# Attention sandwich kernel: a head pair's slot in two stretches instead of three, with seven ring tiles

## The chip, the cores and the metric

The kernel runs on one core of one Trainium2 chip. The metric is the time of one launch on the device, in microseconds (us). Before the change three runs gave 1004.36, 1004.42 and 1005.59 us, so the median is 1004.42 us. One more execution was profiled.

## The reference

The input x has 4 batches of 1024 tokens of 128 numbers, all fp32. Two sublayers follow each other, each wrapped in layer norms and a residual:

```python
x = x + layernorm(attention(layernorm(x)))
x = x + layernorm(ffn(layernorm(x)))
# attention: layer norm with gain and bias, then 16 heads of 64
q, k, v = (xn @ w + b for each)              # 1024 x 64 per head
scores = q @ k.T / 8
scores = where(tril(ones, k=-1), -inf, scores)   # a query sees keys at or after its own place
h = softmax(scores) @ v
out = h @ w0 + b0 + residual
# ffn: 8 experts of rank 16; gates from the first token of each sequence of 64, top 2, softmax
```

The attention is nearly all of the work: 4 batches x 8 pairs of heads = 32 head pairs, each with a triangle of 1024 x 1024 scores for two heads.

## The kernel before

One loop of 32 **slots**, one for each head pair t. The engines are programmed by hand, each with its own instruction list, and are tied by semaphores. The lists of all engines follow the same tables (`TILES`, `T_STEPS`, `BLOCKS`, `S_STEPS`, `ORDER`, `fills`), which therefore set the order of the whole kernel.

For each pair the scores are computed twice. **First scores** (`score`, L649, called S steps, nine a pair): q by k in one product, into banks of the tile `sc` (three PSUM banks, taken in rotation, one for each of the two heads of a step). VectorE takes row maxima from them (`maxima`, L1156 where the mask must be added, L1159 elsewhere) and they are thrown away. The maxima become a shift for each query: `least_of_two` (DVE L1167), `shifts` (POOL L446 and L447), a transpose on TensorE ("m", L755), a copy on ScalarE (L1015), two DMAs that move it into `shift_row` (`move_shift`, L342). They are made a pair or two ahead. **Second scores** (`score_t`, L678 and L683, called T steps, ten a pair): transposed, with high and low parts of q and k (three products), the shift added by a product with `shift_row` (L678). They go to the two PSUM tiles `st0` and `st1` alternately, so step s needs the exponential of step s-2 to be done. ScalarE takes the exponential (`exponentials`, L969) into an SBUF tile. TensorE multiplies the tile with v (`weigh`, L698, called W here) into `po`, and GpSimd adds the tiles up for the softmax's sums (`add`, L467). S steps are written here S0 to S8 and T steps T0 to T9; S0' and so on are those of the pair after the next one's first steps.

Of the ten tiles of a pair, eight go to a ring of five tiles, and the first tile of each half (steps 0 and 7) goes straight to `total`, where the others are added onto it in place. That is why `add` waits for the W of step 0 or 7.

A slot has three **stretches**. Each is: T steps with S steps between them (the letters of `ORDER`), then **fills** (other products, whose results other engines take away), then the W of the stretch's T steps. With the names of `fills`:

| stretch | T and S steps | fills | W of |
|---|---|---|---|
| 0 | S3 T0 S4 T1 T2 S5 | sum(t-1), q(t+2), out(t-2) | T0 to T2 |
| 1 | S6 T3 T4 S7 T5 T6 S8 | k(t+2) | T3 to T6 |
| 2 | S0' T7 S1' T8 T9 S2' | m(t+1), v | T7 to T9 |

"sum" turns GpSimd's totals into one row (L708), which goes through four DMAs to VectorE's reciprocal (L1337), through DRAM and two DMAs (`spread_sums`, L355 and L359) into `inv_row`, and there GpSimd's `normalise` (L474) makes `o_norm`; "out" (L761) multiplies that with w0, and VectorE adds it to `acc` (L1222). Once a batch there are further fills, z, u, logit, mix and up, which turn the normed input of the next batch or do the second sublayer of the last one, and layer norms whose statistics VectorE makes with `norm_stats` (L1129 to L1136) at fixed places of the slots. SyncE issues all DMAs from one queue in program order: in a slot the sums, the reciprocals, the spread, loads of x and the store of a result where there are any, and last the shift.

## Time and profile before

| what | value |
|---|---|
| median of three runs | 1004.42 us |
| the profiled execution | 1005.35 us |
| its span, first to last instruction | 1003.5 us |
| TensorE busy | 963.6 us, 96% |
| VectorE busy | 645.9 us, 64% |
| ScalarE busy | 538.0 us, 54% |
| GpSimd busy | 703.1 us, 70% |
| mean granted TensorE clock | 0.993 |

The profiled execution took 0.93 us more than the median, of which 1.85 us lie outside its span. A busy share is an average over the whole program; what the change does is decided inside a slot, so slots are read one by one. In the timeline a row gives the start, the duration, the engine, the line and the operation; rows of the same kind are merged, and x is their number. Matmuls overlap each other, so what a step takes on TensorE is the distance from its start to the next step's start.

### The profile page before, as it was taken

What the parts mean: (1) busy time and instruction counts of PE and PEld (TensorE: products, weight loads), DVE (VectorE), ACT (ScalarE), POOL (GpSimd) and SP (SyncE); (2) the same over time, 40 slices, a digit from 0 to 9 for tenths busy, and PEclk for the clock granted to TensorE, in tenths of its full rate; (3) what the DMA queues carried; (4) which work ended last, traced back from release to release, by engine and by line L of the source; (5) the groups of instructions that cost most, each with busy time, mean ns of one, the idle gap of its engine ahead of it and who ended that gap; (6) DMA issues with size and microseconds to landing.
All of it is one profiled execution on the core that took longest, in us unless ns stands there. A gap on an engine that the chain in (4) does not pass through costs nothing.

```text
span 1003.5 us, 20485 instructions
## 1 busy us (share of the span) xinstructions
PE 963.6 (96%) x7677; PEld 603.8 (60%) x7682; DVE 645.9 (64%) x1935; ACT 538.0 (54%) x732; POOL 703.1 (70%) x519
## 2 busy tenths in 40 slices
PE   8999999999999999999999999999999999999995
PEld 3465666666666665666665566566666656666563
DVE  4766566565567667657667757656665765756377
ACT  6245655564544565665455565565545546455443
POOL 7266767687666768876576977776687776777752
PEclk9899999999999999999999999999999999999999
DMA  4001101001111100012001210000101210000010
GB/s 114 22 2 24 23 2 23 24 23 44 23 23 26 20 23 23 23 23 45 17 8 23 65 24 23 23 17 8 44 22 24 64 24 14 12 23 23 23 44 21
DMA packets 61809, 26.94 MB, mean 27 GB/s; under 512 B 39056, under 2 KB 53776, under 8 KB 61712
## 3 DMA queue, kind: packets, MB, share of 16 engines
q1 hardware_dynamic: 61712, 25.64, 10.9%
q8 instruction: 61, 1.00, 0.4%
q14 instruction: 36, 0.29, 0.1%
HBM read 22.76 MB, written 2.35 MB: 25 GB/s over the span
## 4 chain that ended last, share of the span: by engine, by line
PE 75%; POOL 11%; DVE 6%; ACT 5%; issue 3%; DMA 0%; POOLq 0%; ACTq 0%; DVEq 0%
PE po L698 21%; PE st L683 15%; PE st L614 9%; POOL total L467 8%; PE sc L649 8%; PE st L761 5%; PE st L678 5%; ACT ring L969 3%; PE sc L708 3%; PE st L629 2%; DVE sc L1156 2%; PE st L630 1%; PE st L631 1%; POOL moments L438 1%; DVE stats L1129 1%
## 5 line engine op out<-in xcount | busy, mean ns | idle before, releaser
L467 POOL TENSOR_TENSOR total<-total,ring 128x1024 f32<-128x1024 f32 (+1 forms) x313 | 539.4, 1723 | 251.6 <-PE po L698 208.6
L1156 DVE CUSTOM_DVE_ANT_0 sc<-sc,key_mask 128x512 f32<-128x512 f32 (+1 forms) x496 | 230.3, 521 | 144.8 <-PE sc L649 142.4
L969 ACT ACTIVATE ring<-st 128x1024 f32<-128x1024 f32 (+1 forms) x256 | 228.7, 919 | 166.3 <-PE st L683 148.3
L1159 DVE TENSOR_REDUCE least<-sc 128x1 f32<-128x512 f32 x268 | 170.2, 677 | 74.6 <-PE sc L649 70.6
L698 PE MATMUL po<-ring,v_sb 128*64 128x512 f32 (+3 forms) x1280 | 210.7, 467 | 0.0
L683 PE MATMUL st<-q_high,k_low 64*128 64x512 f32 (+3 forms) x768 | 177.0, 447 | 0.0
L698 PEld LDWEIGHTS po<-ring,v_sb 128*64 128x64 f32 x1280 | 86.7, 137 | 129.2 <-issue 124.1
L649 PE MATMUL sc<-k_high,q_high 64*128 64x512 f32 (+3 forms) x768 | 135.3, 383 | 11.3 <-DVE least L1156 5.2
L683 PE MATMUL st<-q_low,k_high 64*128 64x512 f32 (+3 forms) x768 | 136.9, 343 | 0.0
L683 PE MATMUL st<-q_high,k_high 64*128 64x512 f32 (+3 forms) x768 | 136.3, 342 | 0.0
L649 PEld LDWEIGHTS sc<-k_high,q_high 64*128 64x128 f32 x768 | 68.8, 185 | 82.4 <-issue 65.9
L678 PE MATMUL st<-shift_row,pick 64*128 64x512 bf16 (+3 forms) x640 | 105.6, 316 | 0.2 <-ACT total L969 0.2
L969 ACT ACTIVATE total<-st 128x1024 f32<-128x1024 f32 x64 | 65.7, 1027 | 54.5 <-PE st L683 54.5
L983 ACT COPY o_raw<-po 128x512 f32<-128x512 f32 x64 | 37.4, 585 | 90.7 <-PE po L698 90.4
L683 PEld LDWEIGHTS st<-q_high,k_high 64*128 64x128 f32 x768 | 76.3, 185 | 6.7
L1208 DVE SCALAR_TENSOR_TENSOR q_low<-st,bias_col,q_high 128x1024 fp32r<-128x1024 f32 x32 | 41.1, 1283 | 60.6 <-ACT q_high L1007 58.5
L683 PEld LDWEIGHTS st<-q_high,k_low 64*128 64x128 f32 x768 | 78.3, 190 | 0.0
L683 PEld LDWEIGHTS st<-q_low,k_high 64*128 64x128 f32 x768 | 77.0, 187 | 1.7
L474 POOL TENSOR_TENSOR o_norm<-o_raw,inv_row 128x1024 f32<-128x1024 f32 x31 | 74.0, 2386 | 3.5 <-DMA inv_row<-sums_dram 3.5
L1156 DVE DVE_READ_ACCUMULATOR2_ANT least<- 128x1 f32 x496 | 69.9, 141 | 0.0
L698 PE MATMUL po<-total,v_sb 128*64 128x512 f32 x256 | 69.3, 620 | 0.0
L761 PEld LDWEIGHTS st<-w_sb,o_norm 128*128 128x128 f32 x480 | 58.0, 191 | 4.2 <-ACT ring L969 1.9
(170 smaller groups left out, 1281.2 us busy)
## 6 DMA issues: line engine op xcount, KB each, us to landing
inv_row<-sums_dram SPq DMA_DIRECT2D x62, 256.0 KB, 4.0
x_a<-x SPq DMA_DIRECT2D x4, 512.0 KB, 5.2
sums<-sums_row SPq DMA_DIRECT2D x124, 2.0 KB, 2.1
x_b<-x SPq DMA_DIRECT2D x3, 512.0 KB, 5.5
out<-res_b SPq DMA_DIRECT2D x3, 512.0 KB, 4.5
ring<-w_pairs SPq DMA_DIRECT2D x1, 1152.0 KB, 7.3
shift_row<-shift_t SPq DMA_DIRECT2D x64, 4.0 KB
x_a<-x SPq DMA_DIRECT2D x2, 256.0 KB, 3.2
```

Source lines behind the costliest of these rows:

```text
L467: nc.gpsimd.tensor_tensor(so_far, so_far, tile_of(n, s)[:, :, col:col + w], ALU.add).then_inc(s_add, 1)
L474: nc.gpsimd.tensor_tensor(o_norm[:], o_raw[n % 2][:], inv_row[:], ALU.mult).then_inc(s_norm, 1)
L614: last = nc.tensor.matmul(dst, low if part == 1 else high, (x_high if part else x_low)[:, tokens], start=(part == 0), stop=(part == 2))
L649: last = nc.tensor.matmul(banks[h][:, col:col + w], q_high[n % 3][rows[h], i * P:(i + 1) * P], k_high[n % 3][rows[h], k0:k0 + w], start=Tr ...
L678: nc.tensor.matmul(st[s % 2][:, h, col:col + w], picked[rows[h], :], shift_row[n % 2][rows[h], q0:q0 + w], start=(i == 0), stop=False)
L683: last = nc.tensor.matmul(st[s % 2][:, h, col:col + w], k[rows[h], keys], q[rows[h], queries], start=False, stop=(part == 2 and i + 1 == l ...
L698: last = nc.tensor.matmul(po[h * D:(h + 1) * D, 0:w], v_sb[(n // 2) % 2][:, j, c0:c0 + D], tile_of(n, s)[:, h, col:col + w], start=(s in F ...
L761: last = nc.tensor.matmul(at("out", n, 0)[:, t * P:(t + 1) * P], o_norm[:, t * P:(t + 1) * P], w0_sb[:, n % PAIRS, :], start=True, stop=True)
L969: nc.scalar.activation(tile_of(n, s)[:, :, 0:w], st[s % 2][:, :, 0:w], ACT.Exp, scale=SCALE).then_inc(s_exp, 1)
L1156: last = nc.vector.tensor_tensor_reduce(bank[:, col:col + w], bank[:, col:col + w], key_mask[:, 0:w], -1.0, 3e38, ALU.add, ALU.min, least[ ...
L1159: last = nc.vector.tensor_reduce(least[:, h, a:a + 1], bank[:, col:col + w], AX.X, ALU.max, negate=True)
L1208: nc.vector.scalar_tensor_tensor(out=low[n % 3][:], in0=src, scalar=bias_col[:, n % PAIRS, w:w + 1], in1=high[n % 3][:].bitcast(fp32), op0 ...
```

## The change

The slot has two stretches. Nothing that is computed changes.

| stretch | T and S steps | fills | W of |
|---|---|---|---|
| 0 | S3 T0 S4 T1 T2 S5 T3 T4 S6 T5 S7 T6 S8 | sum(t-1), q(t+2), k(t+2) | T0 to T6 |
| 1 | S0' T7 S1' T8 T9 S2' | m(t+1), v, out(t-2) | T7 to T9 |

The ring has seven tiles. Tile 0 goes to the ring too, and GpSimd's first addition writes tile 0 + tile 1 to a `total_first` of its own; tile 7 (`IN_PLACE`) goes to the single `total_second` and is added onto in place. `normalise` comes before the additions of tiles 8 and 9 on GpSimd, and `shifts` after all additions of stretch 0. The fills z, u and up take two `sc` banks each, one after the other, instead of an `st` tile. On VectorE a stretch's `take` comes before its layer norm statistics.

```diff
-    T_STEPS = [range(0, 3), range(3, 7), range(7, 10)]
+    T_STEPS = [range(0, 7), range(7, 10)]
...
-    ORDER = ["STSTTS", "STTSTTS", "STSTTS"]
+    ORDER = ["STSTTSTTSTSTS", "STSTTS"]
...
-    FIRST_ORDER = ["TSTSTSS", "STSTTSTS", "STSTTS"]
-    RING = 5
+    FIRST_ORDER = ["TSTSTSTSTSTSTSS", "STSTTS"]
+    RING = 7
...
+    IN_PLACE = 7
+    IN_RING = [s for s in range(STEPS) if s != IN_PLACE]
...
         if g == 0:
-            if 2 <= t < N:
-                found.append((("out", t - 2, 0), y))
-            if 1 <= t < N:
-                found.insert(0, (("sum", t - 1, 0), "sc"))
...
+            if t >= 1:
+                found.append((("sum", t - 1, 0), "sc"))
+            if t + 2 < N:
+                found += [(("q", t + 2, 0), x), (("k", t + 2, 0), y)]
+            if t == N - 1:
+                found.append((("out", t - 2, 0), x))
...
+            if t + 2 < N:
+                found.append((("v", (t + 2) // 2, t % 2), x))
+            if 2 <= t < N - 1:
                 found.append((("out", t - 2, 0), y))
+            if before and i == 5:
+                found.append((("z", c + 1, 0), "sc"))
...
         def tile_of(n, s):
-            if s in FIRST:
-                return total[:, FIRST.index(s), n % 2]
-            return ring[:, ring_count(n, s) % RING]
+            return total_second[:] if s == IN_PLACE else ring[:, ring_count(n, s) % RING]
...
             def add(n, s):
                 half = half_of(s)
                 pool.wait_ge(s_exp, STEPS * n + s + 1)
-                pool.wait_ge(s_pv, STEPS * n + FIRST[half] + 1)
+                if half:
+                    pool.wait_ge(s_pv, STEPS * n + IN_PLACE + 1)
...
+                    nc.gpsimd.tensor_tensor(so_far, tile_of(n, 0) if s == 1 else so_far, tile_of(n, s)[:, :, col:col + w],
+                                            ALU.add).then_inc(s_add, 1)
...
+                    if g == 1 and t >= 1:
+                        normalise(t - 1)
                     for s in T_STEPS[g]:
                         if s in SUMMED and (t, s) not in LAST_SUMS:
                             add(t, s)
-                        if s == 4 and t < N - 1:
-                            shifts(t + 1)
-                    if g == 1 and t >= 1:
-                        normalise(t - 1)
+                    if g == 0 and t < N - 1:
+                        shifts(t + 1)
...
-                    if t >= 0:
-                        place = 3 * i + g
+                    for use, bank in fills(t, g):
+                        take(use, bank)
+                    for place in ((3 * i, 3 * i + 1), (3 * i + 2,))[g]:
```

TensorE's list, inside slot 8, from T2 on. L678 and L683 are a T step, L649 an S step, L708 the sum, L614 a projection. Before:

```order
L678 MATMUL st<-shift_row,pick 128x512 x2
L683 MATMUL st<-q_high,k_low 128x512 x2
L683 MATMUL st<-q_low,k_high 128x512 x2
L683 MATMUL st<-q_high,k_high 128x512 x2
L649 MATMUL sc<-k_high,q_high 128x512 x2
L708 MATMUL sc<-total,ones 32x512 x4
L614 MATMUL st<-x_low,wqk_high 128x512
L614 MATMUL st<-x_high,wqk_low 128x512
L614 MATMUL st<-x_high,wqk_high 128x512
```

The same place now, where L701 and L706 are a T step and L672 is an S step:

```order
L701 MATMUL st<-shift_row,pick 128x512 x2
L706 MATMUL st<-q_high,k_low 128x512 x2
L706 MATMUL st<-q_low,k_high 128x512 x2
L706 MATMUL st<-q_high,k_high 128x512 x2
L672 MATMUL sc<-k_high,q_high 128x512 x2
L701 MATMUL st<-shift_row,pick_masked 128x128 x2
L701 MATMUL st<-shift_row,pick 128x128 x2
L706 MATMUL st<-q_high,k_low 128x256 x2
L706 MATMUL st<-q_low,k_high 128x256 x2
L706 MATMUL st<-q_high,k_high 128x256 x2
L701 MATMUL st<-shift_row,pick 128x512 x2
```

After S5 the short T3 and then T4 follow at once, where there were the sum, a projection, out and the W of three tiles.

GpSimd's list in slot 9, from the shift on, before (L446 and L447 are the shift, L467 an addition, L474 `normalise`):

```order
L446 CAST shift<-least 128x2x8
L447 TENSOR_TENSOR shift<-least,shift 128x2x8
L467 TENSOR_TENSOR total<-total,ring 128x1024
L467 TENSOR_TENSOR total<-total,ring 128x2x384
L467 TENSOR_TENSOR total<-total,ring 128x2x128
L474 TENSOR_TENSOR o_norm<-o_raw,inv_row 128x1024
L467 TENSOR_TENSOR total<-total,ring 128x2x384
```

And in slot 8 now, where L462 and L463 are the shift, L488 an addition, L454 and L455 a layer norm's root, L496 `normalise`:

```order
L488 TENSOR_TENSOR total_first<-total_first,ring 128x2x384
L488 TENSOR_TENSOR total_first<-total_first,ring 128x2x128
L462 CAST shift<-least 128x2x8
L463 TENSOR_TENSOR shift<-least,shift 128x2x8
L454 TENSOR_TENSOR moments<-moments,minus_half 128x8
L455 TENSOR_TENSOR moments<-moments 128x8
L496 TENSOR_TENSOR o_norm<-o_raw,inv_row 128x1024
L488 TENSOR_TENSOR total_second<-total_second,ring 128x2x384
```

The shift now stands behind all additions of tiles 1 to 6, and `normalise` ahead of those of tiles 8 and 9.

VectorE's list at the end of slot 9, from the maxima of S2' on. Before, the out's addition had been done in stretch 0 (L1159 is a maximum, L1129 to L1136 are `norm_stats`):

```order
L1159 TENSOR_REDUCE least<-sc 128x1 x2
L1129 BN_STATS stats<-acc 128x6 x4
L1132 BN_AGGR moments<-stats 128x2 x4
L1135 TENSOR_SCALAR moments<-moments 128x4
L1136 TENSOR_SCALAR moments<-moments 128x4
```

Now, where L1178 is a maximum, L1245 the addition of out, L1148 to L1155 `norm_stats`, and L1175 the maxima of the next slot's S3:

```order
L1178 TENSOR_REDUCE least<-sc 128x1 x2
L1245 TENSOR_TENSOR acc<-st,acc 128x1024
L1148 BN_STATS stats<-acc 128x6 x4
L1151 BN_AGGR moments<-stats 128x2 x4
L1154 TENSOR_SCALAR moments<-moments 128x4
L1155 TENSOR_SCALAR moments<-moments 128x4
L1175 ISA sc,least<-sc,key_mask 128x384
```

The statistics stand behind the addition of out, which is filled late in the slot, and directly ahead of the next slot's first maxima.

## Rows read from the trace of the kernel before

**Rows 1.** Waits: engine line <- for whom: us in total, times, longest.

```profile
PE sc L649 <- DVE least L1156: 5.2, 5, 1.7
PE st L678 <- DVE k_low L1208: 3.5, 4, 1.1
PE sc L708 <- POOL total L467: 3.0, 4, 1.1
```

**Rows 2.** Windows, slot 8: us, then busy us of each engine.

```profile
276.93:305.35 28.42, 28.10 (x231) 17.70 (x229) 18.13 (x55) 14.34 (x17) 19.87 (x14) 1.00 0.10 21
```

**Rows 3.** Timeline of TensorE, slot 8, stretch 0: start, us, engine, line.

```profile
276.93 0.51 PE L649 MATMUL sc<-k_high,q_high 64*128 64x384 f32 x4
277.28 0.39 PE L678 MATMUL st<-shift_row,pick 64*128 64x512 bf16 x2
...
278.50 0.49 PE L649 MATMUL sc<-k_high,q_high 64*128 64x512 f32 x2
...
280.67 0.43 PE L649 MATMUL sc<-k_high,q_high 64*128 64x512 f32 x2
281.03 1.06 PE L708 MATMUL sc<-total,ones 128*32 128x512 f32 x8
...
285.39 1.08 PE L698 MATMUL po<-total,v_sb 128*64 128x512 f32 x4
```

**Rows 4.** Timeline of TensorE, slot 8, stretch 1 and the start of 2.

```profile
288.12 0.50 PE L649 MATMUL sc<-k_high,q_high 64*128 64x256 f32 x4
288.46 0.23 PE L678 MATMUL st<-shift_row,pick_masked 64*128 64x128 bf16 x2
...
288.99 0.39 PE L678 MATMUL st<-shift_row,pick 64*128 64x512 bf16 x2
...
289.92 0.40 PE L649 MATMUL sc<-k_high,q_high 64*128 64x512 f32 x2
290.15 0.23 PE L678 MATMUL st<-shift_row,pick_masked 64*128 64x128 bf16 x2
...
292.25 0.45 PE L649 MATMUL sc<-k_high,q_high 64*128 64x384 f32 x4
292.63 0.50 PE L614 MATMUL st<-x_low,wqk_high 128*128 128x512 f32 x1
...
294.22 3.23 PE L698 MATMUL po<-ring,v_sb 128*64 128x256 f32 x20
297.38 0.50 PE L649 MATMUL sc<-k_high,q_high 64*128 64x512 f32 x2
```

**Rows 5.** Timeline of TensorE, slot 31, which has no S steps: T1 and T2.

```profile
948.49 0.39 PE L678 MATMUL st<-shift_row,pick 64*128 64x512 bf16 x2
...
949.77 0.39 PE L678 MATMUL st<-shift_row,pick 64*128 64x512 bf16 x2 [0.18 <-ACT total L969]
```

**Rows 6.** Timeline of VectorE, slot 8: the maxima of S6, first head.

```profile
288.66 0.43 DVE L1156 CUSTOM_DVE_ANT_0 sc<-sc,key_mask 128x256 f32<-128x256 f32 x1 [1.38 <-PE sc L649]
...
289.39 0.14 DVE L1156 DVE_READ_ACCUMULATOR2_ANT least<- 128x1 f32 x1
```

**Rows 7.** Timeline of VectorE and GpSimd: statistics beside GpSimd's work.

```profile
303.63 0.17 DVE L1135 TENSOR_SCALAR moments<-moments 128x4 f32<-128x4 f32 x1
...
332.66 0.93 DVE L1135 TENSOR_SCALAR moments<-moments 128x4 f32<-128x4 f32 x1
...
331.19 2.37 POOL L474 TENSOR_TENSOR o_norm<-o_raw,inv_row 128x1024 f32<-128x1024 f32 x1
```

**Rows 8.** Timeline of SyncE, slot 8; landing of its spread; a page line: KB, us.

```profile
290.43 0.37 SPq L355 DMA_DIRECT2D sums_dram<-inv_sums  x1
293.14 1.31 SPq L359 DMA_DIRECT2D inv_row<-sums_dram  x2
...
DMA to landing us min/median/max: 3.7/3.8/4.0
...
sums<-sums_row SPq DMA_DIRECT2D x124, 2.0 KB, 2.1
```

171 lines of the change are left out of this document (89 added, 82 removed).

## The prediction, written before the changed kernel ran

> **What bounds the kernel now.** First the page: TensorE is busy 96% of the span, the others 54 to 70% (the table of the profile). So the question is what TensorE's list waits for. The waits view answers for the whole program: TensorE's largest waits are 5.2 us on VectorE's maxima, 3.5 us on VectorE's k_low and 3.0 us on GpSimd's totals [rows 1]. Then one ordinary slot, the eighth: 28.42 us, TensorE busy for 28.10 [rows 2]. Its timeline shows steps that follow each other at the pace of the products. Only one place in it waits: S4 starts 1.57 us after S3, where S3 and T0 take 0.35 and 0.93, so 0.3 us are a wait for VectorE [rows 3]. TensorE's own pace sets the end, then, and a change helps by giving it less to do and hurts by making it wait.
>
> **What it no longer has to do.** Each change of the kind of product costs a little. An S step between T steps takes 0.23 (289.92 to 290.15); S6 behind a W takes 0.34, S5 ahead of the sum 0.36 [rows 3, 4]. A projection is 1.59 between an S step and a W, and six matmuls at 0.23 are 1.38 [rows 4]. The W of 1536 columns takes 2.73 us and that of 1792 takes 3.16 (285.39 to 288.12, 294.22 to 297.38), so a column takes 1.68 ns, 1536 of them 2.58, and 0.15 us are fixed [rows 3, 4]. Where stretches 0 and 1 become one, one each of these goes: 0.11 + 0.13 + 0.21 + 0.15 = 0.6 us a slot. In the 29 slots from 1 to 29 that is -17.4 us. The number of matmuls stays, and out, k, u, z and up only move. The Trainium skill (TensorEngine Tiling (Array Packing), Key Properties) says that a change of the tiling mode drains TensorE; the sum would be the same, as the rows give the price and the page has none.
>
> **What it now waits for in the long stretch.** Seven T steps and six S steps follow each other, where the fills and W of 7 us used to let the other engines catch up. Two loops decide.
>
> ScalarE: a T step needs the exponential of the step two before. Slot 31 has no S steps, and there T1 takes 1.28 us where a T of this width takes 0.93 (288.99 to 289.92), so the loop is 0.93 + 1.28 = 2.21 us [rows 4, 5]. T1, T2 and S5 are 2.09, so T3 waits 0.12. T2, S5 and T3 (0.53 [rows 4]) are 1.69, 1.81 with that wait, so T4 waits 0.4. Later T steps are 2.3 us or more apart. Together 0.52.
>
> VectorE: S(k+1) needs the maxima of the first head of S(k), and the sum needs those of S7's second head. S3 to S4 is 1.57 [rows 3], and S6 has the same two pieces to a head (0.73 from its first maximum to the read of the second [rows 6]). S6 takes 0.12 less than S3, so S7 is 1.45 behind S6, while S6 and T5 (1.06) are 1.29: wait 0.16. An S step that was waited for takes 0.31 and not 0.23, another 0.08. S7 to S8 is about even. The sum comes one S step (0.38) after S8 and needs the head that VectorE takes after the one S8 needed, some 0.65 later: wait 0.27. Together 0.52, an estimate from these rows.
>
> So 1.04 us a slot, x 29 = +30.2. The bounds: nothing, if VectorE and ScalarE run ahead, and 1.6 if each T step must wait for a whole exponential. I take the value worked out, as the loop of 2.21 is measured.
>
> **Waits that go.** The q and k fills now stand 5.7 us of W ahead of T7, and VectorE takes them ahead of its statistics, so the k_low waits (3.5) go. The sum comes 9.4 us into the slot and not 4.1, so GpSimd's totals are ready (3.0). The waits for maxima (5.2) were VectorE being late at the head of a slot, for z or for statistics; I take them out and count what stands there now below. -11.7 [rows 1].
>
> **VectorE late at the head of a slot.** This is the largest new term after the long stretch. In slots 8, 9, 11, 16, 17, 19, 25 and 27 VectorE has statistics in the last stretch, now behind the out it must add. Taking S0' as zero, from the rows of slot 8: the rest of the scores is 3.6 us, m and v 1.9, out 1.9, so out is filled at 7.4, added at 8.8, and the two TENSOR_SCALAR of the statistics come at about 10.1; the next slot starts at 9.7 and its maxima should start at 10.3. GpSimd stands before `normalise`, which needs inv_row: the reciprocal ends at 2.0, the spread is issued 2.7 after the store of the reciprocals (290.43 to 293.14), its second DMA 0.7 after its first and lands 4.0 after its issue [rows 8], at 9.4. So `normalise` runs from 9.4 to 11.8. A TENSOR_SCALAR takes 0.17 us with GpSimd idle, but the one at 332.66, within `normalise`, takes 0.93 and ends with it [rows 7]. Here it would start 0.7 into it and end at 11.9, and the maxima start at 12.0 in place of 10.3. S4 is then 1.7 us late: x 8 = +13.6. Both ends: 0 if out or inv_row come at another time, 3.6 if the second TENSOR_SCALAR also waits for the addition that follows.
> By the Trainium skill (SBUF — State Buffer, Who interferes with whom) a tensor_scalar in a two-port mode and GpSimd shut each other out for a whole instruction, and whoever comes first wins. By that rule the wait is the remainder of `normalise`, as I counted; had VectorE come first, it would be nothing.
> In stretch 0 of the slots with two statistics in a row (six) VectorE ends some 0.45 late for S0': +2.7, from nothing to three times that.
>
> **z.** Three times a program z is filled at a slot's end, now in `sc` banks that the next S3 needs. ScalarE's two passes in halves and VectorE's end about 3.7 us behind the fill, and only 2.3 of W cover it: +4.2, from 2 to 6.
>
> **The shift's DMA.** The reciprocal is behind S0', so SyncE has issued the spread only at 6.1 after S0' (4.7, and 1.3 for its two issues [rows 8]), and m is ready at 4.6: the shift leaves 1.5 us later than it could. Its second DMA, 0.7 later, lands at 8.9 if it takes the 2.1 of the small DMAs of the sums [rows 8], and T0 needs it at 10.1. In ordinary slots 1 us is to spare. In slots 6, 14 and 22 a load of x of 512 KB stands between; if the shift's packets come behind it, T0 is late by 0.85, of which 0.3 is the wait of S4 that was there anyway: +1.7. In slots 9, 17 and 25 the same falls under the late maxima. In the Trainium skill (DMA: Bandwidth & Descriptors, Queues, rings and completion order) descriptors of a ring are taken in order, which gives this wait; no row here has a shift behind a load, and without the order it would be nothing.
>
> **Ends.** Slot 0: fewer kinds, VectorE-bound before and after: -0.5. Slots 30 and 31 have hardly any S steps and no projections; there m waits for GpSimd's shift, T0 to T6 run at the exponentials' pace, and the last sums start later: +3.1, from 0 to 7.
>
> **Sum.** -17.4 + 30.2 - 11.7 + 13.6 + 2.7 + 4.2 + 1.7 - 0.5 + 3.1 = +25.9. The profiled execution took 1005.35, 0.93 above the median, so 1031.2 there and 1030 against the median of 1004.42.
>
> **Rivals.** (1) Faster: TensorE's own time goes on binding. Its place is T2 to T4 and S6 to the sum. If VectorE and ScalarE run ahead there, neither 30.2 nor the statistics' 13.6 and 2.7 arises: 1005.35 - 17.4 - 11.7 + 4.2 + 1.7 - 0.5 + 3.1 = 984.8. For it: 46% of ScalarE's and 36% of VectorE's time is idle, and GpSimd's additions no longer wait for a W. Against it: the loop of 2.21 is latency and not load. It turns faster than before where the waits of the stretch are under 0.15 us a slot with the other terms as they are. Chance 0.13.
> (2) The statistics do not meet `normalise`: 1031.2 - 16.3 = 1014.9. For it: the meeting rests on two chains that end 0.7 us apart. Chance 0.2.
> (3) GpSimd becomes the bound. `normalise`, three additions of the last half and six of the first now run in one piece from 9.4 after S0', and only then the shift: GpSimd's work of a slot is 19.87 us in 14 instructions [rows 2], some 21.5 with the gaps between them, and it starts about where the slot does, while m needs the shift at 22.9. If it is 1 us later than m each slot, +28: 1059. Against it: 1.4 us to spare. Chance 0.09.
> (4) The change doesn't do what it says: not seen, the lists have the order of the table.
> The forecast has 0.58.
>
> **Range and chances.** The forecast's own range is 1018 to 1042: 0.25 us a slot either way in the long stretch is 7 us, and the statistics give as much. With rival 2 and the near side of rival 3 it is 1006 to 1045; rival 1 lies outside. Two us, 0.2%, is what a measurement of this kernel tells from no change. Faster takes rival 1, 0.13; the same 0.04, from rival 2's low end and a milder rival 1; slower 0.83.
>
> **What would show it.** In the changed profile an ordinary slot is about 28.9 us. From S3 to the sum it is 9.3 to 9.6 us, with T4 0.4 late and the sum on VectorE's maxima in the waits view. The merged W is 5.7 us, and no k_low wait is left. In the slots after those eight S4 starts over 3 us behind S3, with a TENSOR_SCALAR of 1.5 to 2 us ahead of it. The prediction is wrong if S3 to the sum is under 8.8 us, if those S4 are in time, or if m waits for GpSimd.

## The result, and the profile after

The changed kernel took 1044.25, 1047.69, 1048.45 and 1050.17 us, median 1048.07; beside it the kernel before took 1005.0 (1004.36 to 1005.9). The ratio is 1.042, with a 95% interval of 1.040 to 1.044. The forecast was 1030 and its range ended at 1045: the direction was right, the size was not. The profiled execution is the fastest of the four, 1044.25 us with a span of 1042.5, so the profile explains 39.0 us of span and not the last 4 us between the medians.

The waits view of TensorE after (columns as in [rows 1]):

```profile
PE st L701 <- DMA shift_row<-shift_t: 14.1, 8, 4.1
PE st L701 <- ACT ring L987: 8.9, 33, 0.6
PE sc L672 <- DVE least L1175: 5.7, 4, 2.2
PE st L652 <- ACT ring L987: 4.7, 25, 0.2
PE st L772 <- POOL o_norm L496: 3.6, 1, 3.6
PE st L701 <- ACT total_second L987: 3.5, 1, 3.5
PE sc L672 <- DVE x_low L1235: 3.5, 3, 1.2
PE sc L672 <- DVE least L1178: 2.6, 5, 0.8
PE sc L827 <- ACT shift_t L1033: 2.4, 3, 0.8
PE sc L830 <- ACT shift_t L1033: 2.3, 3, 0.8
```

The k_low waits of [rows 1] and those of the sum for GpSimd's totals are gone. At the top stands a wait that the kernel before did not have: T0 waiting for the shift's DMA, eight times (in slots 2, 7, 10, 15, 18, 23, 26 and 29).

The windows of slot 8, as [rows 2]:

```profile
280.44:309.29 28.85, 28.12 (x231) 17.96 (x229) 17.70 (x51) 14.20 (x17) 19.65 (x13) 1.00 0.08 20
```

The ordinary slot went from 28.42 to 28.85 us; 28.9 was forecast. The timeline of TensorE in its long stretch, to be read against [rows 3, 4]:

```profile
280.44 0.50 PE L672 MATMUL sc<-k_high,q_high 64*128 64x384 f32 x4
...
284.16 0.42 PE L672 MATMUL sc<-k_high,q_high 64*128 64x512 f32 x2
284.55 0.23 PE L701 MATMUL st<-shift_row,pick_masked 64*128 64x128 bf16 x2
...
285.47 0.39 PE L701 MATMUL st<-shift_row,pick 64*128 64x512 bf16 x2 [0.22 <-ACT ring L987]
...
286.40 0.40 PE L672 MATMUL sc<-k_high,q_high 64*128 64x256 f32 x4
...
287.87 0.50 PE L672 MATMUL sc<-k_high,q_high 64*128 64x512 f32 x2
...
289.87 0.62 PE L731 MATMUL sc<-total_first,ones 128*32 128x512 f32 x2
```

From S3 (280.44) to the sum (289.87) it is 9.43 us, within the 9.3 to 9.6 of the forecast; T4 (285.47) is the step that waits for an exponential, as forecast. S6 to S7 (286.40 to 287.87) is 1.47, the pace of VectorE's maxima (1.45 forecast).

So the loss is elsewhere, at the heads of some slots. TensorE in slot 18, where it was worst, and the windows with the granted clock (the number after the five engines):

```profile
582.49 0.50 PE L672 MATMUL sc<-k_high,q_high 64*128 64x384 f32 x4
587.05 0.61 PE L701 MATMUL st<-shift_row,pick 64*128 64x512 bf16 x2 [4.07 <-DMA shift_row<-shift_t]
```

```profile
585.30:592.20 6.90, 5.15 (x26) 3.40 (x28) 1.29 (x2) 2.05 (x2) 4.64 (x4) 0.51 0.07 21
...
401.02:404.43 3.41, 3.12 (x14) 2.19 (x16) 2.19 (x8) 0.56 (x1) 3.03 (x3) 0.50 0.02 5
889.90:896.00 6.10, 3.92 (x34) 2.64 (x32) 5.40 (x16) 2.62 (x4) 5.54 (x4) 1.00 0.01 3
```

TensorE stood 4.07 us for the shift, up to 587.05. From 585.3, while it stood, to 592.2 the clock was at half, 1.2 of 2.4 GHz, so T0 took 1.68 us in place of 0.93. Slot 18 took 35.08 us. In slot 12, where TensorE had waited 2.03 us for the maxima, it was at half for 3.4 us (second row); at the head of slot 28, after 2.17 us, it stayed at full (third row).

SyncE's list ahead of slot 18 (start, duration of the issue) shows why the shift is late:

```profile
577.77 2.51 SPq L375 DMA_DIRECT2D inv_row<-sums_dram  x2
580.33 0.59 SPq L403 DMA_DIRECT2D out<-res_b  x1
580.97 0.58 SPq L346 DMA_DIRECT2D x_b<-x  x1
581.64 1.97 SPq L358 DMA_DIRECT2D shift_row<-shift_t  x2
```

The spread waits for the late reciprocal, then a store and a load of 512 KB go first. In the trace the packets of the store and the load run from 582.2 to 586.2, those of the shift from 586.1 to 586.4.

The statistics met `normalise` in two of the eight slots only. VectorE and GpSimd at the end of slot 11, where they did, and VectorE at the end of slot 9, where they did not (as [rows 7]):

```profile
398.09 2.22 DVE L1154 TENSOR_SCALAR moments<-moments 128x4 f32<-128x4 f32 x1
...
397.92 2.37 POOL L496 TENSOR_TENSOR o_norm<-o_raw,inv_row 128x1024 f32<-128x1024 f32 x1 [3.80 <-PE po L721]
```

```profile
338.53 0.17 DVE L1154 TENSOR_SCALAR moments<-moments 128x4 f32<-128x4 f32 x1
...
338.69 0.57 DVE L1175 CUSTOM_DVE_ANT_0 sc<-sc,key_mask 128x384 f32<-128x384 f32 x1
```

At 398.09 the small instruction came 0.17 us behind `normalise` and ended with it, 2.22 us later. In slot 9 it came 29.2 us after the slot's first product, 0.55 us ahead of `normalise` (339.08).

Last, slot 30. ScalarE there stood 8.76 us for VectorE's gate work, whose small instructions stood in turn beside GpSimd's additions:

```profile
971.35 0.40 ACT L1014 ACTIVATE up_gated<-up_sb,gate 128x128 f32<-128x128 f32 x1 [8.76 <-DVE gate L1213]
```

```profile
967.12 2.26 DVE L1208 TENSOR_TENSOR gate<-gate 128x8 f32<-128x8 f32 x1
969.42 0.17 DVE L1209 TENSOR_TENSOR gate<-gate,own 128x8 f32<-128x8 f32 x1
```

The account, each term of the forecast beside what the two profiles show. Slots 1 to 29 went from 842.63 to 876.38 us; the measured terms are sums over the slots in which the thing stands, less an ordinary slot. The waits that go are not measured by themselves: that row is what is left over in slots 1 to 29, whatever its cause.

| term | forecast, us | profile, us |
|---|---|---|
| long stretch less the kinds that go, 29 x 0.43 | +12.8 | +12.5 |
| shift's DMA, half clock after it included | +1.7 | +17.1 |
| statistics beside GpSimd at a slot's end | +13.6 | +5.4 |
| z in `sc` banks | +4.2 | +3.7 |
| m ahead of logit and mix | none | +3.0 |
| two statistics in stretch 0 | +2.7 | +2.8 |
| waits that go | -11.7 | -10.8 (the remainder) |
| up to the end of slot 0 | -0.5 | -3.0 |
| slots 30, 31 and the tail | +3.1 | +8.3 |
| sum | +25.9 | +39.0 |

The -3.0 is the luck of two executions and not the change. It stands ahead of S3 of slot 0, in windows with nearly the same work (columns as in [rows 2], before and then after):

```profile
0.00:48.77 48.77, 43.28 (x191) 20.02 (x195) 29.81 (x82) 19.71 (x33) 24.00 (x61) 0.93 0.25 70
```

```profile
0.00:45.84 45.84, 39.88 (x193) 18.88 (x194) 29.82 (x82) 19.71 (x33) 24.21 (x62) 1.00 0.27 74
```

In the profile of the kernel before the clock was at half from 23.6 to 30.4 us, in that of the changed kernel it was not; in e1 and e2 below, which begin like the changed kernel, it was, and S3 of slot 0 starts at 48.66 and 48.87. Without this difference the two spans would be some 42 us apart, an estimate from these rows, near the 43 us between the medians. The other executions have no trace, so that it accounts for the rest is not shown.

### The profile page after: what moved, and what is told of

It is laid out like the page before. It is cut to its first block, busy times and chain, and to the rows that moved or that the text cites. A ratio compares the mean times of both kernels' runs of the same rounds, so it can differ in the third digit from the quotient of the medians.

```text
span 1042.5 us, 20498 instructions
## 1 busy us (share of the span) xinstructions
PE 967.0 (93%) x7682; PEld 612.7 (59%) x7682; DVE 653.7 (63%) x1938; ACT 536.3 (51%) x741; POOL 705.4 (68%) x519
## 3 DMA queue, kind: packets, MB, share of 16 engines
q1 hardware_dynamic: 61712, 25.64, 10.8%
## 4 chain that ended last, share of the span: by engine, by line
PE 62%; DVE 15%; ACT 7%; DMA 6%; POOL 4%; issue 3%; SPq 2%; POOLq 0%; ACTq 0%; DVEq 0%
PE po L721 18%; PE st L706 11%; PE st L637 9%; DVE sc L1175 8%; PE sc L672 5%; ACT ring L987 5%; PE st L701 4%; PE st L784 4%; PE sc L731 3%; DMA shift_row<-shift_t 3%; DMA sums_dram<-inv_sums 3%; PE st L652 2%; SPq L375 1%; POOL total_first L488 1%; PE po L841 1%
## 5 line engine op out<-in xcount | busy, mean ns | idle before, releaser
L488 POOL TENSOR_TENSOR total_first<-total_first,ring 128x1024 f32<-128x1024 f32 x188 | 343.9, 1829 | 25.5 <-POOL total_first L488 0.9
L987 ACT ACTIVATE ring<-st 128x1024 f32<-128x1024 f32 (+1 forms) x288 | 258.6, 929 | 130.5 <-PE st L706 124.8
L1175 DVE CUSTOM_DVE_ANT_0 sc<-sc,key_mask 128x512 f32<-128x512 f32 (+1 forms) x496 | 229.5, 521 | 64.0 <-PE sc L672 62.5
L1178 DVE TENSOR_REDUCE least<-sc 128x1 f32<-128x512 f32 x268 | 170.3, 678 | 129.2 <-PE sc L672 127.7
L721 PE MATMUL po<-ring,v_sb 128*64 128x512 f32 (+3 forms) x1408 | 232.7, 478 | 0.0
L496 POOL TENSOR_TENSOR o_norm<-o_raw,inv_row 128x1024 f32<-128x1024 f32 x31 | 73.5, 2371 | 226.2 <-DMA inv_row<-sums_dram 185.9
L721 PEld LDWEIGHTS po<-ring,v_sb 128*64 128x64 f32 x1408 | 96.1, 137 | 148.2 <-issue 143.2
L706 PE MATMUL st<-q_high,k_low 64*128 64x512 f32 (+3 forms) x768 | 180.6, 454 | 0.0
L672 PE MATMUL sc<-k_high,q_high 64*128 64x512 f32 (+3 forms) x768 | 135.6, 383 | 19.9 <-DVE least L1175 5.7
L706 PE MATMUL st<-q_low,k_high 64*128 64x512 f32 (+3 forms) x768 | 138.4, 344 | 0.0
L706 PE MATMUL st<-q_high,k_high 64*128 64x512 f32 (+3 forms) x768 | 137.6, 345 | 0.0
L488 POOL TENSOR_TENSOR total_second<-total_second,ring 128x768 f32<-128x768 f32 (+2 forms) x93 | 119.3, 1283 | 19.1 <-issue 11.5
L701 PE MATMUL st<-shift_row,pick 64*128 64x512 bf16 (+3 forms) x640 | 107.4, 322 | 22.8 <-DMA shift_row<-shift_t 14.1
L672 PEld LDWEIGHTS sc<-k_high,q_high 64*128 64x128 f32 x768 | 72.0, 185 | 79.3 <-issue 44.2
L1245 DVE TENSOR_TENSOR acc<-st,acc 128x1024 f32<-128x1024 f32 x30 | 36.7, 1225 | 92.8 <-PE st L784 92.8
L488 POOL TENSOR_TENSOR total_first<-ring 128x1024 f32<-128x1024 f32 x32 | 76.2, 2382 | 17.9 <-ACT ring L987 13.8
L706 PEld LDWEIGHTS st<-q_high,k_high 64*128 64x128 f32 x768 | 77.8, 187 | 7.7
L706 PEld LDWEIGHTS st<-q_low,k_high 64*128 64x128 f32 x768 | 79.0, 190 | 2.7
L706 PEld LDWEIGHTS st<-q_high,k_low 64*128 64x128 f32 x768 | 80.2, 193 | 0.0
L1175 DVE DVE_READ_ACCUMULATOR2_ANT least<- 128x1 f32 x496 | 70.2, 141 | 0.0
```

The costliest lines, as they stand in the source:

```text
L488: nc.gpsimd.tensor_tensor(so_far, tile_of(n, 0) if s == 1 else so_far, tile_of(n, s)[:, :, col:col + w], ALU.add).then_inc(s_add, 1)
L496: nc.gpsimd.tensor_tensor(o_norm[:], o_raw[n % 2][:], inv_row[:], ALU.mult).then_inc(s_norm, 1)
L672: last = nc.tensor.matmul(banks[h][:, col:col + w], q_high[n % 3][rows[h], i * P:(i + 1) * P], k_high[n % 3][rows[h], k0:k0 + w], start=Tr ...
L701: nc.tensor.matmul(st[s % 2][:, h, col:col + w], picked[rows[h], :], shift_row[n % 2][rows[h], q0:q0 + w], start=(i == 0), stop=False)
L706: last = nc.tensor.matmul(st[s % 2][:, h, col:col + w], k[rows[h], keys], q[rows[h], queries], start=False, stop=(part == 2 and i + 1 == l ...
L721: last = nc.tensor.matmul(po[h * D:(h + 1) * D, 0:w], v_sb[(n // 2) % 2][:, j, c0:c0 + D], tile_of(n, s)[:, h, col:col + w], start=(s in F ...
```

## The experiments

Theory at this point: the long stretch costs what was forecast, and the rest is collisions at the slot's ends that can be moved apart. Rivals: the shift's late DMA is a matter of SyncE's order alone; the ring and the totals cost it, not the two stretches; VectorE's order costs it, whatever the number of stretches; or the long stretch is dearer than it looks.

**Loads behind the shift (e1_loads_last).** In SyncE's program the shift goes ahead of the loads of x and the store.

```diff
+                if t < N - 1:
+                    move_shift(t + 1)
...
-                if t < N - 1:
-                    move_shift(t + 1)
```

> The changed kernel, where SyncE issues the shift's two DMAs ahead of a slot's load of x and store of a result. Theory: the shift's packets queue behind the loads' (in the changed profile TensorE waits 14.1 us for the shift in 8 slots, and the clock falls after the two longest). Then these waits all but go: about 1034, 12 to 16 us less than the changed kernel. Rival: the shift is late because the spread itself holds SyncE; then it is late by as much: 1045 to 1048. Second rival: T0 would have waited for VectorE anyway (as the prediction had it): under 3 us gained.

Measured: 1041.79 us (1037.52 to 1048.6), ratio 1.038 (1.032 to 1.044; the kernel before took 1003.51 beside it and the next three). None of the three numbers expected came. Its profiled execution, 1045.38, has one wait for the shift left, 1.21 us in slot 2, but

```profile
PE sc L672 <- DVE least L1175: 15.0, 8, 2.9
```

where the changed kernel has 5.7 in 4. Two things brought these waits. In this execution the statistics met `normalise` ahead of five slots (10, 12, 18, 20 and 26) and not of two; in the changed kernel's profile VectorE had been in time in slots 10, 18 and 26, so the wait for the shift had covered nothing there. And the edit has a cost of its own: x is loaded later now, and ahead of slot 1 the statistics wait for it.

```profile
79.76 0.87 DVE L1148 BATCH_NORM_STATS2 stats<-x_a 128x6 f32<-128x128 f32 x4 [4.79 <-DMA x_a<-x]
```

Slot 1 took 32.13 us in place of 27.12. Slots 1 to 29 together are 1.7 us shorter than in the changed kernel, near what the three give together: 16.1 less for the shift, 5.0 more for slot 1 and 8.6 more for the meetings, so 2.5 less. So SyncE's order is a cause of the waits for the shift. What it is worth in the median is not shown: the medians differ by 6 us, but the four executions differ by 11 us, and the intervals of the two ratios overlap.

**The reciprocal in stretch 0 (e2_reciprocal_early).** VectorE does it at the end of stretch 0 and not between the maxima of S0' and S1'.

```diff
-                        if (g, k) == (1, 0) and t >= 1:
-                            dve.wait_ge(s_sums, 64 * t)
-                            reach(dve, s_inv_out, 16 * (t - 1))
-                            nc.vector.reciprocal(inv_sums[:], sums[:]).then_inc(s_inv, 1)
...
+                    if g == 0 and t >= 1:
+                        dve.wait_ge(s_sums, 64 * t)
+                        reach(dve, s_inv_out, 16 * (t - 1))
+                        nc.vector.reciprocal(inv_sums[:], sums[:]).then_inc(s_inv, 1)
```

> The changed kernel, with VectorE's reciprocal behind its takes in stretch 0 and not behind the maxima of S0'. Inverse sums are then spread some 5 us earlier. Theory: both the shift's DMA and the chance meeting of normalise with the statistics at the slot's end go: 1026, with runs that differ by less than 1 us. Rival: only the DMA waits go and the meeting stays, since normalise then starts when out is filled, 2 us ahead of the statistics: 1034, with runs still several us apart.

Measured: 1036.96 us (1036.37 to 1038.45), ratio 1.034 (1.032 to 1.035). The 1026 expected failed, since the meeting stayed; so did the rival's runs that lie several us apart. The waits for the shift are gone, SyncE's order being the old one, and the runs now agree within about 2 us. All eight slots behind statistics are long, 30.35 to 30.45 us each: with the fixed meeting the loss of 1.5 us is there every time. GpSimd and VectorE at the end of slot 9:

```profile
337.60 2.37 POOL L496 TENSOR_TENSOR o_norm<-o_raw,inv_row 128x1024 f32<-128x1024 f32 x1 [6.17 <-PE st L784]
339.92 2.64 POOL L488 TENSOR_TENSOR total_second<-total_second,ring 128x768 f32<-128x768 f32 x2
```

```profile
337.47 1.22 DVE L1245 TENSOR_TENSOR acc<-st,acc 128x1024 f32<-128x1024 f32 x1 [2.54 <-PE st L784]
...
340.05 1.74 DVE L1154 TENSOR_SCALAR moments<-moments 128x4 f32<-128x4 f32 x1
```

Both engines are released by the same products, out's (L784): `normalise` because they have read o_norm, VectorE because it adds their result. So the two always keep step, and the instruction that shuts the statistics out is the addition behind `normalise`, which began 0.13 us before (the row holds two; the first ends at 341.75). In the changed kernel inv_row lands later and in most of the eight slots `normalise` starts when it does. That is from 0.17 us ahead of the first of the two small instructions to 0.97 behind it, so a few tenths of a us decide whether they meet.

The account holds here too. In slots 1 to 29 it gives 17.1 less for the shift and 6.8 more for eight meetings in place of two, so 10.3 less; the profiles differ by 11.3 (865.11 against 876.38).

**Fills moved (e3_fills_moved).** The fills of stretch 1 in the order m, v, z, out, logit, mix.

```diff
-            if after and i == 5:
-                found.append((("logit", c - 1, 0), "sc"))
-            if after and i == 6:
-                found.append((("mix", c - 1, 0), "sc"))
...
+            if after and i == 5:
+                found.append((("logit", c - 1, 0), "sc"))
+            if after and i == 6:
+                found.append((("mix", c - 1, 0), "sc"))
```

and "out" likewise behind z.

> The changed kernel, with the fills of stretch 1 in the order m, v, z, out, logit, mix. Theory: z's passes on ScalarE and VectorE then lie beside out as well as W, and logit and mix no longer wait for the copy of m out of the sc bank: 3 x 1.2 and 5 x 0.6 us less, so about 6 to 7 us less than the changed kernel, 1041. Rival: the waits move to the next slot's S3 (logit and mix now hold banks that S3 needs): no gain.

Measured: 1040.62 us (1037.44 to 1044.58), ratio 1.037 (1.034 to 1.040), 7.4 less than the change. The number is the expected one, the way to it only in part. In the profile 3.5 us are in slots 1 to 29, where three meetings stand against two, and 3.1 in slot 30. Slot 5 fell from 30.97 to 29.76, as z is covered by out; m is taken before logit and mix need its bank. In slots 13 and 21 z's wait only moved, from S3 to the logit (1.71 us for x_low in each).

**W of two tiles inside the long stretch (e4_w_inside).** The W of tiles 0 and 1 stands behind S5, so that VectorE and ScalarE can catch up there.

```diff
+                        if place_of == 5:
+                            for s in range(early):
+                                weigh(t, s)
...
-                    for s in T_STEPS[g]:
+                    for s in T_STEPS[g][early:]:
```

> The changed kernel, with the W of tiles 0 and 1 behind S5, inside the long stretch. Theory of the two loops: T3 and T4 wait 0.5 us a slot for exponentials; the 1.7 us of W give ScalarE that time, and the W costs 0.25 for the two more changes of kind: the ordinary slot falls from 28.85 to 28.6, the time by 8 us to 1040. Rival: the stretch is bound by VectorE's maxima from S6 on; then the ordinary slot stays or grows by 0.25, 1048 to 1056.

Measured: 1047.88 us (1044.01 to 1050.45), ratio 1.044 (1.041 to 1.047). The ordinary slot fell to 28.6, as expected, and nothing came of it in the median, where 1040 was expected. Waits of its TensorE:

```profile
PE st L701 <- DMA shift_row<-shift_t: 12.9, 9, 3.6
PE sc L672 <- DVE least L1182: 8.5, 8, 2.2
```

The slot's own 0.25 us came back as waits for the maxima at the slots' ends and heads. That the chains over VectorE, GpSimd and the DMAs did not get shorter would explain it; it was not tried. The statistics also met `normalise` ahead of four slots in this execution, two of them only for its last us.

**The kernel before with the new ring (e5_before_ring7).** Three stretches, with seven ring tiles, `total_first` and `total_second`, and the additions free of W.

```diff
-    RING = 5
+    RING = 7
...
-        total = sb("total", [P, 2, 2, 2, HALF])
+        total_first = sb("total_first", [P, 2, 2, HALF])
+        total_second = sb("total_second", [P, 2, HALF])
```

> The kernel before (three stretches) with only the other half of the change: seven ring tiles, tile 0 in the ring, total_first and total_second apart, the additions' waits that go with them. Theory: the loss is all from the two stretches; here the ordinary slot stays at 28.4 and the 3.0 us that the sum waits for GpSimd go, as GpSimd can start adding before the W: 1001 to 1003, against 1004. Rival: the single total_second or the ring costs something itself: over 1008.

Measured: 1007.65 us (1005.65 to 1009.7) against 1004.11, ratio 1.0035 (1.0022 to 1.0048). The expectation failed: the ring brings nothing, and costs 3.5 us. An ordinary slot stays at 28.42, but slots 3, 9, 11, 15, 17, 19, 23 and 25 are at 29.3, with

```profile
PE st L689 <- DVE k_low L1217: 7.4, 8, 0.9
```

where [rows 1] has 3.5 in 4. VectorE and GpSimd ahead of such a k_low, in slot 9:

```profile
326.22 1.68 DVE L1144 TENSOR_SCALAR moments<-moments 128x4 f32<-128x4 f32 x1
...
327.88 1.27 DVE L1217 SCALAR_TENSOR_TENSOR k_low<-st,bias_col,k_high 128x1024 fp32r<-128x1024 f32 x1
```

```profile
325.51 2.36 POOL L477 TENSOR_TENSOR total_first<-total_first,ring 128x1024 f32<-128x1024 f32 x1
```

The additions, free of the W, come at other times, and one of them stands beside the statistics that are ahead of k_low. So in three stretches the ring accounts for 3.5 of the +43, and is no gain.

**The kernel before with takes first (e6_before_takes_first).** Three stretches, and only VectorE's order changed: takes ahead of the statistics.

```diff
+                    for use, bank in fills(t, g):
+                        take(use, bank)
...
-                    for use, bank in fills(t, g):
-                        take(use, bank)
```

> The kernel before with VectorE's takes of a stretch ahead of its layer norm statistics, as in the change. Theory: the 3.5 us of waits for k_low go and nothing is made late: 1001, against 1004. Rival: the statistics then end later and the next maxima wait for them: no change.

Measured: 1036.7 us (1033.29 to 1044.44), ratio 1.033 (1.030 to 1.036), the largest miss of all: +33 us with TensorE's list untouched. Its longest waits, and VectorE and GpSimd at the end of stretch 1 of slot 9:

```profile
PE sc L649 <- DVE least L1156: 18.6, 8, 4.3
```

```profile
328.50 1.97 DVE L1135 TENSOR_SCALAR moments<-moments 128x4 f32<-128x4 f32 x1
...
328.08 2.37 POOL L467 TENSOR_TENSOR total<-total,ring 128x1024 f32<-128x1024 f32 x1
```

The statistics wait for the take of k, then stand beside an addition, and the maxima of S0' begin 2 us late, at 330.46. The largest part is elsewhere, though: slots 14 and 22 took 37.7 and 37.9 us in place of 31.0. There VectorE's gate work for the second sublayer stands behind the takes, beside two additions, and the maxima begin 4.3 us late; the longest of its instructions, in slot 14:

```profile
470.16 2.36 DVE L1182 TENSOR_TENSOR rank<-rank,earlier 128x64 f32<-128x64 f32 x1
```

So the time of the kernel before hangs on where these few small instructions stand. The same edit is in the change, in two stretches, and no run takes it back there as a whole. So the rival about VectorE's order is not excluded. e9 below takes a part of it back and gains 9.4 us over e2, but e10 gains 15.7 with that order as it is, by filling out earlier.

**Narrow maxima (e7_changed_narrow_maxima and e8_before_narrow_maxima).** VectorE takes the maxima of S steps over 128 columns and not all, and the exponential's scale is smaller so that nothing overflows; the row maxima of the other columns are left out. VectorE should then be no bound in the stretch, and only ScalarE's loop be left.

```diff
-                            last = nc.vector.tensor_reduce(least[:, h, a:a + 1], bank[:, col:col + w], AX.X, ALU.max,
+                            last = nc.vector.tensor_reduce(least[:, h, a:a + 1], bank[:, col:col + P], AX.X, ALU.max,
```

> The changed kernel, where each of VectorE's maxima over the first scores reads only 128 columns, and the exponentials' scale is 4096 times smaller so that they stay finite (the shift and the weights are thus not the reference's). Theory of the two loops: the wait of S4 (0.37) and those of S7, S8 and the sum (0.52) go and the exponentials' 0.52 stay: the ordinary slot goes from 28.85 to about 27.95. Rival: VectorE costs the long stretch nothing of its own: 28.5.

> The kernel before with the same two edits (maxima over 128 columns, the smaller scale). Theory: only the wait of S4 goes, 28.42 to 28.05 a slot, so that the two kernels' ordinary slots come within 0.1 us of each other: what is left to the changed one is 0.6 us saved on changes of kind and 0.52 spent on exponentials. Rival: 28.42 as before.

Measured in one execution each: 1006.26 and 993.85 us. The slot 8 of the changed and of the unchanged kernel:

```profile
271.74:299.61 27.87, 27.45 (x233) 17.87 (x231) 11.54 (x51) 14.21 (x17) 20.35 (x14) 1.00 0.11 21
```

```profile
272.15:300.10 27.95, 27.76 (x231) 17.57 (x230) 12.52 (x55) 14.35 (x17) 19.86 (x14) 1.00 0.09 21
```

With VectorE's share taken out, the slot in two stretches is shorter by 0.08 us than the one in three; with it, longer by 0.43. So VectorE's loop costs 0.98 us of slot in the one and 0.47 in the other. That is the difference of 0.52 that the forecast gave to VectorE, and the 0.6 less 0.52 of kinds and ScalarE. The programs as a whole are 12 us apart here, where it was 39: the pace of the slots is 29 x 0.51 = 15 of the difference, slots 30, 31 and the tail are 4, and most of the rest is that the kernel before fell by only 8.8 us in slots 1 to 29, where its pace alone would give 13.6. The 12 us that stay hold the shift, z and the ends, which narrow maxima leave in place.

**Statistics ahead (e9_statistics_ahead).** Beside this one and the next three the kernel before took 1005.58. On the early reciprocal: the statistics of stretch 1 of a batch's first and fourth slot stand before the takes, and no longer behind them.

```diff
+                    if (i, g) in ((0, 1), (3, 1)):
+                        statistics(c, 3 * i + 2)
```

> The changed kernel with the early reciprocal, and now also with VectorE's layer norm statistics of stretch 1 ahead of its takes in the first and the fourth slot of a batch (places 2 and 11; the third fixed place stays behind them). With the early reciprocal alone eight slots met normalise, each at +1.5 us, and it took 1036.96. Theory (what those slots cost is VectorE's small TENSOR_SCALAR shut out by normalise, because the statistics stand behind the late addition of out): of the eight slots five have their statistics at the moved places and should fall from 30.4 to 28.9 us, three stay at 30.4; 1036.96 - 5 x 1.5 = 1029.5, range 1027.5 to 1031.5, and the waits of TensorE for maxima of 1.5 us or more go from ten to about five. Rival A (the late maxima come from out's addition itself, which is behind the fills whatever the statistics do): the eight slots keep 1.5 us each, 1036 to 1038. Rival B (the statistics ahead now meet the additions of GpSimd or delay the addition of out, which holds S3 or the next fill): 1.0 us or more comes back in five slots, 1034 or above.

Measured: 1027.52 us (1025.45 to 1029.65), ratio 1.022 (1.020 to 1.023), -9.4 where -7.5 was expected. The five slots are at 28.83 or 28.84 us, the three others at 30.4, and in slots 11 and 19 TensorE waits 0.5 for the maxima at S1'. Slots 1 to 29 are 8.0 us shorter than with the early reciprocal alone; the 3 us more between the two profiles are the clock ahead of slot 0 once more. The slots were chosen and the loss follows them: it is the place of the small instructions.

**Out earlier (e10_out_first).** On the early reciprocal: the fills in the order m, out, v. The text below names the order out, v, m; the kernel that ran leaves m first, so the rival about a late m was not tried.

```diff
+            if 2 <= t < N - 1:
+                found.append((("out", t - 2, 0), x))
+            if t + 2 < N:
+                found.append((("v", (t + 2) // 2, t % 2), y))
...
-            if t + 2 < N:
-                found.append((("v", (t + 2) // 2, t % 2), x))
-            if 2 <= t < N - 1:
-                found.append((("out", t - 2, 0), y))
```

> The changed kernel with the early reciprocal, and the fills of stretch 1 in the order out, v, m (z, logit, mix where they are) in place of m, v, out. The addition of out then comes about 3.4 us earlier on VectorE, and the statistics with it, at some 6.7 us after S0', while normalise starts at about 7.5 to 9.4. Theory (the cost is where in time the two stand): the statistics end before normalise starts, none of the eight slots has the +1.5 us, and 1036.96 - 8 x 1.5 = 1025, range 1022 to 1029; m and with it the shift come 3.4 us later, though, and leave behind x loads in the slots with one, so up to 3 us may come back. Rival A (out waits for o_norm, since normalise of the pair before ends late): TensorE waits at the fill in each ordinary slot, 0.3 us or more in 29 slots, 1033 or above. Rival B (the shift is the tighter chain: m 3.4 us later makes the shift late in every slot): T0 waits in ordinary slots, 28.85 becomes 29.5 or more, and the time is 1040 or above.

Measured: 1021.21 us (1019.48 to 1024.76), ratio 1.016 (1.014 to 1.018). Slots 10, 18 and 26 are at 29.04, the other five at 28.85 to 28.87. But the mechanism that was expected isn't there in the slots ahead of these three. In slot 9:

```profile
334.10 2.39 POOL L496 TENSOR_TENSOR o_norm<-o_raw,inv_row 128x1024 f32<-128x1024 f32 x1 [4.75 <-PE st L784]
```

```profile
336.54 1.81 DVE L1154 TENSOR_SCALAR moments<-moments 128x4 f32<-128x4 f32 x1
```

`normalise` moves with out, since out releases both, and the statistics are shut out for 1.81 us as before. They end at 338.3, though, 0.75 us after S3 (337.59), where in the kernel of the early reciprocal it was 1.4 us later. There the stall remains and has become nearly free. Ahead of the other five slots the small instructions end 0.9 us before S3 and none is stretched.

**All mends (e11_changed_mended).** The changed kernel with the early reciprocal, the loads last, the order m, out, v, logit, mix, z, the statistics ahead, and ScalarE's gate work (`gate_up`) moved to the end of the seventh slot.

> The changed kernel with all the mends at once: early reciprocal, the shift's DMAs ahead of the x loads and stores, fills of stretch 1 in the order m, out, v, logit, mix, z, statistics at places 2 and 11 ahead of the takes, and the gate work of ScalarE half a slot later. What was measured alone: the early reciprocal -11, its meetings with normalise eight times 1.5, fills moved -7.4. Theory (the forecast's accounting: everything above 1005 - 17.4 - 11.7 + 30.2 = 1006 is collisions that can be moved out of the way, beside 3 to 6 us of ends): 1037 - 5 x 1.5 (statistics) - 4 to 7 (z, logit, mix, m) - 1.5 (out earlier) gives 1021 to 1025, range 1016 to 1027, ordinary slot still 28.85. It stays slower than the kernel before, because the long stretch's 0.43 us a slot (12.5 us) can't be moved out of the way. Rival (the long stretch costs nothing when the collisions are gone): 1008 or below. Rival B (mends don't add up, each collision makes room for the next): 1030 or above.

Measured: 1019.51 us (1018.03 to 1023.73), ratio 1.014 (1.012 to 1.017). Slot 30 fell to 23.94 us, from 29.25 in the changed kernel and 28.86 in e10, and TensorE's wait of 3.5 us in it is gone. That this is the gate work is likely and not shown alone, as e3 took 3.1 us out of the slot by its fills. Slot 1 rose to 30.0: there the statistics wait for x to arrive,

```profile
78.41 0.87 DVE L1148 BATCH_NORM_STATS2 stats<-x_a 128x6 f32<-128x128 f32 x4 [4.93 <-DMA x_a<-x]
```

since the load now stands behind the shift. Against e10, slots 1 to 29 are 2.3 us longer and slot 30 is 4.9 shorter. The ordinary slot is 28.87, and two stretches stay 1.4% slower than three.

**The kernel before, statistics apart (e12_before_statistics_apart).** Three stretches; of two statistics in a row the second goes to stretch 0, ahead of the takes there (but not in a batch's second slot), and GpSimd's roots of stretch 2 go behind its additions.

```diff
-                    if t >= 0:
-                        place = 3 * i + g
+                    for place in ((3 * i, 3 * i + 1) if i != 1 else (3 * i,), (3 * i + 1,) if i == 1 else (), (3 * i + 2,))[g]:
```

> The kernel before, with three stretches, and only the place of small operations moved: of the two layer norm statistics in a row, the second goes to stretch 0 ahead of its takes (but not in the second slot of a batch), and GpSimd's roots of stretch 2 come behind its additions of that stretch. TensorE's list is untouched. Theory (the 5.2 us of waits for maxima are VectorE late behind statistics, in five places, and can be taken out in that kernel too): three of the five waits go, -3 to -4 us, 1000 to 1002. Rival A (the statistics in stretch 0 then stand ahead of the takes of q and of out and make those late, as in the kernel before with all takes ahead, where +33 us came back): 1006 or above. Rival B (TensorE's own pace sets everything, waits are only moved): 1003.5 to 1005.

Measured: 998.81 us (997.37 to 1001.11) against 1005.58, ratio 0.993 (0.9915 to 0.9943): faster than both kernels. Slots 1 to 29 went from 842.63 to 837.72 us, slots 11, 19 and 20 from about 29.5 to 28.5, 28.4 and 28.8. Its waits beside [rows 1]:

```profile
PE sc L655 <- DVE least L1162: 3.4, 4, 1.1
...
PE sc L714 <- POOL total L467: 1.7, 5, 0.5
PE st L684 <- DVE k_low L1214: 1.3, 2, 0.7
```

## Why the prediction was wrong, step by step

**What bounds, the kinds, the long stretch: right.** 28.85 us a slot where 28.9 was forecast, 9.43 us from S3 to the sum, the merged W 5.73, no k_low wait. The size of VectorE's loop is shown by the pair with narrow maxima, T4's wait by the timeline: 0.92 from T3 to T4 where 0.53 was without it. VectorE's items in the forecast add up to 0.51 and not 0.52. The forecast also calls the 5.2 us for the maxima TensorE's largest wait and S4's the only one in slot 8. In the kernel before v's fill waited longer in total, 5.6 us in 30 short waits for ScalarE's exponential; in the changed kernel it is 4.7 in 25 (L652), so the slip cost the sum nothing that matters.

**The step that failed: the shift's DMA.** The forecast had the right chain (late reciprocal, late spread, the shift behind a load) and priced it at +1.7; it was +17.1. Three things were mis-sized. First, the slots: the forecast says that in slots 9, 17 and 25 "the same falls under the late maxima" and so puts them at nothing. The maxima were in time there, and these three cost 12.7 us. The three slots that it did price cost 3.3, and two that it didn't have 1.2 (the waits in slots 2 and 29). Second, the queue: ahead of slots 18 and 26 the shift's packets came behind some 4 us of a store's and a load's packets of 512 bytes, and SyncE's issue of the spread took 1.98 to 2.51 us in slots 9, 17 and 25 in place of 1.3 [rows 8]; why it did is open, as it took 1.77 and 1.94 in slots 8 and 16, which have no load. Third, the clock: with the waits of 4.07 and 3.51 us came half speed, 3.6 us more for the steps up to T2 of slots 18 and 26. SyncE's order is only a part of the cause: with the early reciprocal the waits went with the order as it was. The Trainium skill (DMA: Bandwidth & Descriptors, Queues, rings and completion order) has each DMA engine take the descriptors of a ring in order, though a later one may finish its write earlier. The trace agrees ahead of slot 18, with the shift's packets from 586.1 and the last of the load's at 586.2; ahead of slot 26 the shift's run from 830.3 to 830.8 and the last of the load's end at 831.1, so there the two overlap.

The shift and the statistics are best read together, since the forecast let the one hide under the other. The forecast had 15.3 us for the two and the profile has 22.5. That is 7 of the 13 us between forecast and profile; the ends are 5, logit and mix 3, and the start -2.5, which is chance.

**The statistics: the mechanism right, the certainty wrong.** Forecast 8 x 1.7, in the profile two meetings, +5.4, of which 1.3 is half clock in slot 12. The forecast put `normalise` 0.7 us ahead of the statistics in all eight slots; in the profile it starts from 0.17 ahead to 0.97 behind, five times within 0.35. So single executions fall out differently: the profiles of e1, e3 and e4 have five, three and four meetings. The kernel with the early reciprocal fixes the meeting and shows the price, 8 x 1.5 = 12 us. That the spread of the changed kernel's runs (6 us) comes from this is likely, as it is 2 us where the meeting is fixed; the other three executions have no trace, so it isn't shown. The Trainium skill (SBUF — State Buffer, Who interferes with whom) says that a `tensor_scalar` that runs in a two-port mode and a GpSimd instruction exclude each other for a whole instruction, the first to come winning. The rows agree in length: 2.22 and 1.74 us, each to within 0.1 of the end of the GpSimd instruction beside it.

**z right, logit and mix missed.** +3.7 for +4.2. The forecast lets "out, k, u, z and up only move" and has no term for logit and mix. Behind m these need its bank before ScalarE has read it, 0.6 us five times.

**Ends: under-sized.** +8.3 for +3.1, above the 7 that was its upper end. Slot 30 is 2.4 of it: TensorE waits there while ScalarE's gate work waits for VectorE's, and in e11 the slot is 2.9 us shorter than in the kernel before. The other 5.8 are in slot 31 and the tail, where TensorE waits 3.6 us for `o_norm` and the clock is at half from 1005.2 to 1012.0; no experiment aimed at them, and e11 still has 4.7. The start was 2.5 us better than forecast by the clock alone, as said above.

**The rivals.** Rival 1 (TensorE binds) fell: with most collisions moved away the slot is still 28.87, and 27.87 with narrow maxima. Rival 2 (no meeting) was right for six of eight slots, and its 1014.9 was not, for it left the shift where it was. Rival 3 (GpSimd bound) fell: m has no wait for GpSimd in ordinary slots. What stays open: the rest of the median beyond the clock at the start, the 5.8 us in slot 31 and the tail, the change with all statistics ahead of the takes, and how far the mends could still be taken in two stretches.

## What to carry to other kernels

A late small transfer is worth a row of its own for every slot in which a large one may go ahead of it; if the argument says that it hides under another wait, price it also for the case that the other wait does not come, and add the half clock that can come with a long one. Where a forecast rests on two chains that end within a fraction of a us, the case is neither "meets" nor "doesn't": look which event releases both. And when a slot's sum is right and the program's is not, compare the slots one by one: 14 of the 32 were 1.2 us or more longer than before. And look at the clock ahead of the part that was changed, before a difference of 3 us is put down to the change.

## What the runs showed of the hardware that I had not expected

A VectorE `tensor_tensor` of 128 x 8 numbers with both inputs in SBUF took 2.26 us at 967.12 beside GpSimd's additions, and the next of the same size 0.17. So it is not only `tensor_scalar` that is shut out. The Trainium skill (SBUF — State Buffer, Who interferes with whom) states this for two SBUF inputs beside a GpSimd instruction that reads SBUF, and the rows agree. The other small instructions of the layer norms (L1148 took 0.27 to 0.30 us in all 160 cases) and the maxima were not stretched anywhere in the changed kernel.

TensorE's clock went to half at waits of 2.03, 4.07 and 3.51 us in the middle of the program (slots 12, 18 and 26), and not at the 2.17 us of slot 28. In e1 it did at 1.83, 2.12, 2.24 and 2.90 us (slots 12, 20, 18 and 1), and not at 2.31 and 2.16 (slots 10 and 26). So the length of a wait does not tell by itself. The kernel before has no such stretch between its first 31 us and 969 us.

The same start of the same program came out 3 us apart: S3 of slot 0 stands at 45.8 us in the profiles of the changed kernel, e3 and e9, where the clock was never at half before it, and at 48.7 to 48.9 in those of e1, e2 and e4, where it was for 6.8 us.
